# Routed experts of a scan-and-MoE kernel: weight loads cut into 2 KB rows, padding rows left out of the gather, routing weight moved to VectorE

## The reference

```python
aff = sigmoid(einsum('bsd,de->bse', x, wa))
topk_p, topk_i = top_k(aff, 2);  topk_p = topk_p / sum(topk_p)
combine = sum(one_hot(topk_i, 16) * topk_p[..., None], axis=2)
y = gelu(einsum('bsd,edf->bsef', x, rg) + rgb) * (einsum('bsd,edf->bsef', x, rw1) + rb1)
routed = einsum('bsed,bse->bsd', einsum('bsef,efd->bsed', y, rw2) + rb2, combine)
return x + shared + routed          # 2 shared experts, dense
```

## Time and profile before

| what | value |
|---|---|
| median of 3 executions | 881.7 us |
| profiled execution: time, span | 884.4 us, 882.3 us |
| PE busy | 783.9 us (89%) |
| DVE busy | 660.8 us (75%) |
| ACT busy | 557.5 us (63%) |
| POOL busy | 550.5 us (62%) |
| data moved by DMA | 95.57 MB in 35384 packets |

### The profile page before, as it was taken

How to read it: one execution, slowest core, us unless ns; L and a number is a source line. 1 busy time by engine, 2 the same in 40 slices (tenths; PEclk the granted TensorE clock), 3 DMA queues, 4 the chain that set the end, 5 groups by cost and what they waited for, 6 DMA issues and landing times.

```text
span 882.3 us, 16042 instructions
## 1 busy us (share of the span) xinstructions
PE 783.9 (89%) x4358; PEld 589.2 (67%) x4359; DVE 660.8 (75%) x859; ACT 557.5 (63%) x931; POOL 550.5 (62%) x347
## 2 busy tenths in 40 slices
PE   6963799999999988997899999999999998999992
PEld 3622688888888878886777778886555554555551
DVE  4999999999999998999586759544655555556651
ACT  3896899999999999994333431024555554545541
POOL 9651399989999999997815560211444543546532
PEclk9975899999999999999799999999999999999996
DMA  6010311212141122101220121366577867678753
GB/s 182 1 55 0 108 52 58 60 49 61 50 155 49 54 61 92 59 14 49 95 96 1 49 102 42 129 253 275 121 163 226 235 175 223 154 211 205 180 143 48
DMA packets 35384, 95.57 MB, mean 108 GB/s; under 512 B 7760, under 2 KB 8272, under 8 KB 32000
## 3 DMA queue, kind: packets, MB, share of 16 engines
q1 hardware_dynamic: 23360, 65.50, 21.6%
q0 software_dynamic: 11968, 29.37, 15.6%
HBM read 122.24 MB, written 21.36 MB: 163 GB/s over the span
## 4 chain that ended last, share of the span: by engine, by line
PE 43%; DMA 17%; DVE 17%; POOL 9%; issue 7%; ACT 5%; POOLq 1%; DVEq 0%; SPq 0%; ACTq 0%
DVE r L1060 12%; DMA out<-sb_sb,ids 9%; DMA out<-sg,ids 8%; PE ps L1446 6%; PE ps L1448 6%; PE ps L1447 6%; PE ps L1549 5%; POOL r L526 5%; PE ps L1572 5%; PE ps L1550 3%; PE ps L1774 3%; PE ps L1793 2%; DVE r L963 1%; POOL r L599 1%; ACT mem L765 1%
## 5 line engine op out<-in xcount | busy, mean ns | idle before, releaser
L526 POOL TENSOR_TENSOR r<-r,mem 128x1024 f32<-128x1024 f32 x126 | 295.4, 2380 | 34.8 <-DVE r L1060 34.2
L1060 DVE TENSOR_TENSOR_SCAN r<-r,ps 128x1024 f32<-128x1024 f32 x128 | 286.7, 2276 | 9.7 <-issue 9.1
L750 ACT ACTIVATE r<-mem,nega 128x511 f32<-128x511 f32 x256 | 166.9, 714 | 1.8 <-DVE r L1060 1.7
L1549 PE MATMUL ps<-ident,mem 128*128 128x128 f32 x768 | 130.3, 279 | 28.4 <-DVE r L1060 21.7
L1572 PE MATMUL ps<-ident,r 128*128 128x128 f32 x1024 | 132.6, 273 | 1.5 <-POOL r L526 1.3
L765 ACT ACTIVATE mem<-mem,b_turned 128x512 f32<-128x512 f32 x192 | 124.7, 715 | 8.7 <-PE ps L1550 8.3
L1549 PEld LDWEIGHTS ps<-ident,mem 128*128 128x128 f32 x768 | 87.2, 142 | 53.8 <-issue 52.8
L1572 PEld LDWEIGHTS ps<-ident,r 128*128 128x128 f32 x1024 | 115.8, 141 | 2.3 <-POOL r L526 1.8
L1550 PE MATMUL ps<-mem 128*128 128x128 f32 x512 | 99.7, 277 | 0.0
L1793 PE MATMUL ps<-mem 128*128 x188 | 92.2, 615 | 1.8 <-ACT mem L915 1.0
L1446 PE MATMUL ps<-split 128*128 128x512 f32 x216 | 88.2, 408 | 4.8 <-DVE split L1134 2.3
(11 more groups left out here) (205 smaller groups left out, 1304.8 us busy)
## 6 DMA issues: line engine op xcount, KB each, us to landing
r<-in_r_up SPq DMA_DIRECT2D x47, 1024.0 KB
mem<-in_r_down SPq DMA_DIRECT2D x47, 512.0 KB
mem<-cm_rows SPq DMA_DIRECT2D x64, 256.0 KB, 3.3
mem<-in_r_b SPq DMA_DIRECT2D x4, 2048.0 KB, 15.1
out<-acc POOLq DMA_DIRECT2D x17, 256.0 KB, 3.2
r<-in_x SPq DMA_DIRECT2D x4, 1024.0 KB, 4.9
xn_scratch<-r SPq DMA_DIRECT2D x16, 256.0 KB, 2.7
mem<-in_ctx_t SPq DMA_DIRECT2D x4, 512.0 KB, 7.7
```

The lines of the kernel that those rows point to most:

```text
L526: pool.tensor_tensor(state[:, k % 2, ec:ec + 2], state[:, k % 2, ec:ec + 2], c, ALU.mult).then_inc(s["weighed"], 1)
L750: act.activation(decay[:, k % 2, ec, 1:L], delta[:, b, ec, 1:L], ACT.Exp, scale=nega[:, ec, n:n + 1]).then_inc(s["decay_ready"], 1)
L1060: dve.tensor_tensor_scan(state[:, half, ec:ec + 2].rearrange("p e l -> p (e l)"), decay[:, half, ec:ec + 2].rearrange("p e l -> p (e l)"), ...
L1549: pe.transpose(ps[:, ec, lt * P:(lt + 1) * P], dbu_t[:, k % 2, lt, ec * P:(ec + 1) * P], ident[:])
```

## The change

Four edits, all in the routed stage:

1. Each up load becomes four DMAs of 128 rows of 2 KB, each down load two. Every part has the condition and counts the same semaphore, so the waits ask for 4 x 16 and 2 x 16 a block.
2. The gather gets a bounds check: ids of 2048 and above (the padding) move nothing, and the row keeps what an earlier block left in it.
3. ACT's `block_result` is gone. DVE multiplies the routing weight into the hidden rows and, for the bias, computes bias x weight + product. `y_ready` is now set by DVE and replaces `yb_ready`.
4. On DVE `hidden(j)` stands ahead of `add_bias(j-2)`.

```diff
-            def load(weights, r_weights, loaded, j, r):
+            def load(parts, loaded, j, r):
...
-                sp.dma_start(weights[:, ds(slot_j, 1)], r_weights[ds(e, 1)].rearrange("e p n -> p e n"), cond=new).then_inc(s[f"{loaded}_{r}"], 16)
+                for weights, r_weights in parts:
+                    sp.dma_start(weights[:, ds(slot_j, 1)], r_weights[ds(e, 1)].rearrange("e p n -> p e n"), cond=new).then_inc(s[f"{loaded}_{r}"], 16)
...
-                load(up_w, r_up, "up", j, r)
+                load([(up_w[:, :, kc * 2 * F:(kc + 1) * 2 * F], r_up[:, :, kc * 2 * F:(kc + 1) * 2 * F]) for kc in range(KC)], "up", j, r)
...
-                load(down_w, r_down, "down", j, r)
+                load([(down_w[:, :, fc], r_down[:, :, fc * D:(fc + 1) * D]) for fc in range(FC)], "down", j, r)
...
-                                        in_offset=bass.IndirectOffsetOnAxis(ids[:, j:j + 1], 0)).then_inc(
+                                        in_offset=bass.IndirectOffsetOnAxis(ids[:, j:j + 1], 0),
+                                        bounds_check=T - 1, oob_is_err=False).then_inc(
...
-            def block_result(j, r):
-                act.wait_ge(s["yb_ready"], j + 1)
-                act.activation(y_sb[r], y_sb[r], ACT.Copy, scale=row_w[:, ds(j, 1)]).then_inc(s["y_ready"], 1)
...
-                dve.tensor_tensor(hy[:, half], hg[:, half], hb[:, half, F:2 * F], ALU.mult).then_inc(s["hy_ready"], 1)
+                dve.scalar_tensor_tensor(out=hy[:, half], in0=hg[:, half], scalar=row_w[:, ds(j, 1)], in1=hb[:, half, F:2 * F],
+                                         op0=ALU.mult, op1=ALU.mult).then_inc(s["hy_ready"], 1)
...
-                dve.tensor_tensor(y_sb[r], ps[:, 6 + r % 2], tile(b2_all, e), ALU.add).then_inc(s["yb_ready"], 1)
+                dve.scalar_tensor_tensor(out=y_sb[r], in0=tile(b2_all, e), scalar=row_w[:, ds(j, 1)], in1=ps[:, 6 + r % 2],
+                                         op0=ALU.mult, op1=ALU.add).then_inc(s["y_ready"], 1)
```

More of the change, by code:

```diff
@@ L286, in bass_xattn_scan_moe_kernel @@
         uph_made upr_made xgr_made up_0 up_1 up_2 up_3 down_0 down_1 down_2 down_3 xg_0 xg_1 xg_2 xg_3 xgt_ready xgt_copied h_ready
-        hb_ready hg_ready hy_ready hyt_ready hyt_copied o_ready yb_ready y_ready y_even y_odd
+        hb_ready hg_ready hy_ready hyt_ready hyt_copied o_ready y_ready y_even y_odd
         """.split()
@@ L903, in weight_head @@
                 slot_j = act.value_load(blk_slot[0:1, ds(j, 1)], min_val=0, max_val=SLOTS - 1)
-                act.wait_ge(s[f"up_{r}"], 16 * (round_ + 1))
+                act.wait_ge(s[f"up_{r}"], 16 * KC * (round_ + 1))
                 since(act, s["h_ready"], j - 1)
@@ L926, in step @@
                 hidden_gate(j, r % 2)
-                if not isinstance(j, int) or j >= 4:
-                    block_result(j - 2, (r - 2) % RING)
                 turn_hidden(j, r % 2)
-                if isinstance(j, int) and j == 3:
-                    block_result(0, 0)
-                    block_result(1, 1)
             act.wait_ge(s["blocks_ready"], 3)
@@ L947, in _ @@
                 step(j, j // RING, j % RING)
-            for j in range(NBLK - 2, NBLK):
-                block_result(j, j % RING)
         @block.vector
@@ L1406, in step @@
                     token_rest(j + 1, (r + 1) % 2)
+                hidden(j, r % 2)
                 if not isinstance(j, int) or j >= 4:
                     add_bias(j - 2, (r - 2) % RING, round_ + (r - 2) // RING)
-                hidden(j, r % 2)
                 if isinstance(j, int) and j == 3:
@@ L1787, in down @@
                 pe.wait_ge(s["hyt_copied"], j + 1)
-                pe.wait_ge(s[f"down_{r}"], 16 * (round_ + 1))
+                pe.wait_ge(s[f"down_{r}"], 16 * FC * (round_ + 1))
                 if isinstance(j, int) and j == 0:
                     pe.wait_ge(s["so_added"], NT)
-                since(pe, s["yb_ready"], j - 1)
+                since(pe, s["y_ready"], j - 1)
                 for fc in range(FC):
```

## The result

The changed kernel takes 964.18 us (median of 4 executions, 962.5 to 967.1) against 881.41 us for the kernel before (median of 4, 879.24 to 884.68). The ratio is 1.095, with a 95% interval of 1.092 to 1.098: slower by 9.5%. The forecast was 960 us. The profiled execution took 967.1 us, with a span of 964.6.

What follows compares the result with a forecast made beforehand. SP's DMA issuing was taken to bound the changed kernel: block 46's last part at 935.5, plus 5.5, 13 and 11.0 us of tail, made 965, less 5 for quieter table reads: 960 us, range 931 to 992.

Steps and rivals of the forecast that it cites:

- SP has the least room: Routed loop before the change: SP busy 96% of the time, 5.58 us a pair of loads beside PE's 5.4.
- The price of a part: Each further DMA on SP costs 0.49 us skipped, 0.76 taken; 157 parts in the loop add 92.9 us.
- quieter table reads: SP's register reads in slower blocks meet less memory traffic; 5 us taken off the sum.
- Ahead of the loop: Extra parts of the first loads cost 8.9 us; biases start 5.6 us later, SP's loop 7.1 us later, at 617.9.
- The tail: After block 46's last part: 5.5 us to PE's product, 13 to the last scatter (queue gone), 11.0 to the end.
- Every block takes SP's pace: Routed loop: ACT, DVE and PE stand behind SP's issues, not the weights' arrival; a pair takes 7.9 us.
- ACT waits in nearly every block: Sign in the profile after: ACT's weight head waits for the up DMA in nearly every block.
- The clock of TensorE: Rival: idle PE falls to 1.2 GHz for most of the stage, 0.8 us more a block, 994 us; chance 8%.
- What the 2 KB rows give back: Scatters beside weight loads near 4.87 us instead of 9.75; counted as nothing at 7.9 us a block.
- the 14 us of scatter waits: Blocks 14 to 44 before the change: 5.87 us a block instead of 5.4, put down to DVE awaiting landed scatters.
- takes PE out from behind DVE's scatter waits: Product ahead of the bias frees PE from DVE's 31 us of scatter waits; worth 1 to 2 us in the last blocks.
- the first rival: Parts cost under about 0.1 us, SP stays ahead, scatter waits come back: 870 us, median near 868; chance 5%.

Runs made afterwards that it cites:

- e8_light_parts: Changed kernel, all four edits, with SP's three table reads a load packed into one: 903.31 us, ratio 1.024 to the kernel before.
- e5_three_more: Changed kernel with the down load whole again, so only the up load is cut, three DMAs more a block: 944.33 us, ratio 1.073.
- e9_light_rows: Changed kernel with one packed table read, product behind the bias again, and 2 KB rows made by one DMA a load: 874.06 us, ratio 0.9925.
- e11_light_old_order: Changed kernel with whole loads, one packed table read a load, and the product behind the bias of block j-2 again: 873.66 us, ratio 0.991.
- e7_light: Kernel before, with SP's three table reads a load replaced by one read of a packed table: 876.94 us, ratio 0.994.
- e1_whole: Changed kernel with its first edit undone, up and down weights by one DMA each, other three edits kept: 880.24 us, ratio 1.001.
- e10: Changed kernel with whole loads and one packed table read a load, the other three edits kept: 878.13 us, ratio 0.996.
- e4_long_rows: Changed kernel with the same number of load issues but long rows (up 7.25 KB and 256 B, down 3.75 KB and 256 B): 966.27 us, ratio 1.098.

## Why the prediction was right

**SP has the least room.** Right, and in size: 5.65 us of work a pair before, by the measure of the table (the forecast's 5.58 divided the same 223.2 us by 40 pairs, where the 79 steps are 39.5). That four parts more bind it is shown by the dose: 0, 1, 3 and 4 parts more give 5.72, 6.29, 7.28 and 7.82 us a pair, which is 0.52 to 0.57 a part and where the sum of the forecast has 92.9 / 157 = 0.59.

**The price of a part.** 0.49 us skipped and 0.76 taken were predicted from a sum of four instructions and a gap of 0.04. The trace after has 0.48 and 0.73 on average. The loop took 308.7 us where 223.2 + 92.9 = 316.1 was forecast; the two prices explain 98 x 0.01 + 59 x 0.03 = 2.8 us of it. The forecast took another 5 us off for quieter table reads. That term held: added up from the traces, the 237 reads of the loop took 77.4 us before and 70.7 after.

**Ahead of the loop.** The biases' load went out at 590.27 and not 588.3, block 0's up bias was at 605.25 (604.5 forecast), and the loop began at 620.64, forecast 617.9: 2.7 us late.

**The tail.** From the last part of block 46 (about 930.8) to the end of the span it is 33.8 us; 5.5 + 13 + 11 = 29.5 were forecast. Rows of the changed kernel's timeline that answer to the last ones of the earlier trace rows:

```profile
938.46 0.79 PE L1440 MATMUL ps<-acc_again,blk_val_again 128*128 128x512 f32 x1
...
952.15 1.55 POOL L634 DMA_INDIRECT out<-sg,ids  x1 [4.07 <-DMA out<-sg,ids]
954.01 1.55 POOL L634 DMA_INDIRECT out<-sb_sb,ids  x1 [0.30 <-issue]
```

PE starts the last block 7.6 us after the last part and not 5.5, and the last scatters still queue: the one at 952.15 waited 4.07 us for the one before to land. "The queue is gone at a slower pace" was wrong for the last blocks, since they come at 5 us each. The three errors, +2.7, -7.4 and +4.3 us, with the 5 us taken off, leave a span of 964.6 for 960. So the closeness of the sum owes something to errors of opposite sign.

**"Every block takes SP's pace", "ACT waits in nearly every block".** This step was wrong in form and right in its sum. The waits are 16 and not 40, and 15 of them end with a landing, which the forecast had held not to be late. A load that is skipped counts its semaphores at the issue; a load that moves data counts when it has landed. Block 12 shows the first: the head starts 0.3 us after its last skipped issue. In the changed kernel the parts of block 22 go out from 740.33 on, and ACT gets them at 747.21, after a wait of 4.76 us:

```profile
747.21 1.04 ACT L909 CAST acc_again<-r 128x1024 fp32r x1 [4.76 <-DMA r<-in_r_up]
```

The last of the four issues ends at 742.83, so 4.4 of those 6.9 us are the transfer's. Meanwhile SP goes on and gains a lead, and the one or two blocks after it run at PE's own pace, until the lead is used up. DVE's up biases stand 5 to 7 us apart after such a block and up to 15 at it. The mean is SP's pace because SP itself never waits.

**The clock of TensorE.** The rival had 8% and didn't come. The granted clock did fall, as that rival had it, but in the loop it cost nothing, as was argued: SP never waits for PE there, so a slower PE can't have held it up. The busy times, clock, DMA share and GB/s of the loop, first in the kernel before, then in the changed kernel:

```profile
610.00:843.00 233.00, 226.49 (x808) 131.69 (x807) 132.04 (x202) 120.24 (x241) 108.72 (x78) 0.99 0.72 184
...
620.00:930.00 310.00, 250.97 (x820) 140.70 (x818) 139.10 (x204) 94.89 (x205) 108.66 (x79) 0.91 0.58 136
```

The clock goes from 0.99 to 0.91, and PE is busy 24 us longer in the loop for about the same work; the 0.94 of the earlier trace rows is one stretch of 30 us with late scatters, not the loop. e8_light_parts, e5_three_more and the changed kernel all follow SP's work with no term for the clock.

**What the 2 KB rows give back.** "I count nothing" was right, but its reason was too kind: it held that the 14 us of scatter waits would come back in a stage bound by scatters. With SP light and the same order (e9_light_rows and e11_light_old_order) there is no difference, but hardly any scatter wait of DVE was left in either. So whether short rows would bring the 14 us back where the waits are there was not tested. By the Trainium skill ("DMA: Bandwidth & Descriptors", Queues, rings and completion order) a DMA engine changes between queues only at packet boundaries. That the short rows should therefore help was the forecast's inference from it, and no run here shows it. DVE's waits for landed scatters are 8.7 us in e7_light, where they were 34.3 before, with 8 KB rows and only less work on SP. This suggests that they depend on when loads are issued as much as on their rows; that was not tested apart.

**Edits 2 to 4.** Each was counted at nothing behind SP, which e1_whole and the dose can't contradict. POOL's gather with a bounds check takes 1061 ns on average (1055 before), and DVE's 128x512 instruction with a scalar 748 ns, as its nearest row said (691 ns before). The 128x256 one was put at half of that rise and rose more, from 418 to 485 ns; together it is 47 x 0.124 = 5.8 us of work on DVE and not 4, hidden here:

```profile
L601 POOL DMA_INDIRECT r<-xn_scratch,ids x47 | 49.9, 1061 | 39.5 <-PE ps L1754 26.3 <-issue 13.0 <-DVE sg L1392 0.3
...
L1392 DVE SCALAR_TENSOR_TENSOR sg<-mem,row_w,ps 128x512 f32<-128x512 f32 x24 | 17.9, 748 | 13.5 <-issue 7.7 <-PE ps L1787 5.7
```

What the prediction missed is the fourth edit without SP's cover. It said that the product ahead of the bias "takes PE out from behind DVE's scatter waits", and named the rest behind the bias only for the case of a late scatter. The runs show that PE waits for it with hardly a late scatter about: e11 against e10 is 4.5 us, 0.1 a block, more than the 3.3 us that edits 2 and 3 may give beside it. The gather's fewer bytes (91.67 MB in place of 95.57, the 1920 rows of 2 KB) were not measured alone; they and the weight on DVE are the 3.3 us between e7_light and e11_light_old_order. The two intervals overlap, so this gain isn't shown.

**The Trainium skill on issue time** ("DMA: Bandwidth & Descriptors", Issuing engines are not separate DMA queues: "usually small relative to the DMA itself"). This was the first rival. For one DMA that moves data nothing here speaks against it: 0.73 us of issue stands beside the 4.4 us from block 22's last issue to its landing. But 98 of the 157 parts have no DMA behind them and cost 0.48 us each, 47 us, and the 59 taken ones 43 us, all of it on a sequencer that was 96% full. Their sum, less the room that SP had, is what makes the 9.5%.

## What to carry to other kernels

Count the work of the sequencer that issues the DMAs as that of any engine: table reads, address arithmetic, the move and the issue, per item, against the time of an item; it has no busy row on the page, and a list of its waits that is nearly empty is the sign (9.3 us in 232 here). A DMA whose condition is false costs its instructions all the same, so cutting a load into parts multiplies what two of three blocks pay for nothing. If short rows are wanted, let one DMA make them by its layout; and before moving an instruction on an in-order engine, look at what filled the wait that it leaves.

## What the runs showed of the hardware

A further conditional DMA with addresses from registers costs SP 0.48 us on average when skipped and 0.73 when taken (the changed kernel's loop); e4_long_rows, with rows of 256 B and 7.25 KB, has 0.47 and 0.73. Reading a value from a table costs SP 0.27 us for the read (median, up to 1.35 in the kernel before) and some 0.35 for the arithmetic and the check that follow. The up load of block 22, 1 MB cut into four, was there for ACT 6.9 us after its first issue, beside scatters and gathers. Rows of 2 KB and of 8 KB loaded the same weights with no difference in the time of a kernel that has few waits for scatters (874.06 and 873.66 us), and a bounds check on an indirect gather of which a third is skipped left its issue on POOL as long as before (1061 against 1055 ns).
